# The columns of 27 tiles from a second layout of x instead of from TensorE's transposes, and the context's scans ahead of the mask's last part

## The reference, cut to what matters

```python
def _layernorm(x):  return (x - mean(x)) / sqrt(var(x) + 1e-5)
def rmsnorm(x, g):  return x * rsqrt(mean(x*x) + 1e-5) * g

e = _layernorm(x)
h = rmsnorm(e, g_res) @ W_in + b_in                 # 4096 x 512
p = rmsnorm(ctx, g_init)[:, :512]                   # 3202 x 512
s[i] = a * s[i-1] + b * p[i]                        # a scan over 3202 rows
x = x + h + s[plug]                                 # plug: rows picked by the mask's running sum
x = x + gelu(_layernorm(x) @ w1 + b1) @ w2 + b2     # 512 -> 2048 -> 512
```

## Time and profile before

| | us |
|---|---|
| median of 3 runs | 851.08 (849.31 to 851.92) |
| the profiled execution, its own time | 849.29 |
| its span | 847.6 |
| TensorE busy / VectorE / ScalarE / GpSimd | 833.6 / 318.0 / 286.9 / 254.7 |
| matmuls of the second phase | 3072 |
| share of the chain that ended last: TensorE / VectorE / DMA | 88% / 5% / 3% |

### The profile page before, as it was taken

One profiled execution on the slowest core, in us unless ns is written; L12 is line 12 of the kernel. 1 busy time (PEld: TensorE's weight loads), 2 busy tenths in 40 slices (PEclk: granted clock), 3 DMA queues, 4 the chain that ended last, 5 costly groups with the idle time before them and its releaser, 6 DMA issues.

```text
span 847.6 us, 10756 instructions
## 1 busy us (share of the span) xinstructions
PE 833.6 (98%) x3786; PEld 684.8 (81%) x3786; DVE 318.0 (38%) x511; ACT 286.9 (34%) x522; POOL 254.7 (30%) x236
## 2 busy tenths in 40 slices
PE   7999989999999999999999999999999999999998
PEld 5887868888888888888888887888888888888886
DVE  5899762534342333324152425133113311242112
ACT  4674335442532244222622253222222322222221
POOL 2273365970262016300532053203500250001000
PEclk9999999999999999999999999999999999999999
DMA  9877687170215021331215021502300140010001
GB/s 233 253 205 217 218 242 253 49 172 1 74 51 156 16 74 51 93 79 49 73 49 124 0 74 49 97 0 100 50 0 1 50 97 2 0 50 0 1 1 50
DMA packets 34968, 71.07 MB, mean 84 GB/s; under 512 B 5716, under 2 KB 5716, under 8 KB 33176
## 3 DMA queue, kind: packets, MB, share of 16 engines
q1 hardware_dynamic: 25964, 58.91, 21.6%
q0 software_dynamic: 4608, 8.39, 6.3%
q10 hardware_dynamic: 4368, 3.42, 1.3%
HBM read 47.87 MB, written 22.84 MB: 83 GB/s over the span
## 4 chain that ended last, share of the span: by engine, by line
PE 88%; DVE 5%; DMA 3%; SPq 1%; issue 1%; POOL 1%; ACT 0%; DVEq 0%; POOLq 0%; ACTq 0%
PE acc L841 14%; PE acc L842 14%; PE acc L843 14%; PE h_bank L842 14%; PE h_bank L843 14%; PE h_bank L841 14%; DMA xa_odd<-in_x_dram 2%; PE t_bank L900 2%; DMA x_next<-scan_table,idx 1%; DVE h_lo L1023 1%; DVE st_a L1018 1%; DVE cl L1037 1%; POOL x_next L541 1%; DVE xa_odd L1031 1%; PE t_bank L873 1%
## 5 line engine op out<-in xcount | busy, mean ns | idle before, releaser
L1242 DVE TENSOR_TENSOR h_lo<-g_f,h_hi 128x512 fp32r<-128x512 f32 x128 | 101.3, 791 | 449.6 <-ACT g_f L778 440.1
L776 ACT ACTIVATE h_hi<-h_bank,b_c 128x512 fp32r<-128x512 f32 x128 | 88.1, 689 | 441.1 <-PE h_bank L843 436.2
L841 PE MATMUL h_bank<-xt_hi,w_hi 128*128 128x512 f32 x512 | 201.9, 394 | 0.0
L841 PE MATMUL acc<-w_hi,h_hi 128*128 128x512 f32 x512 | 199.8, 390 | 0.0
L843 PE MATMUL h_bank<-xt_hi,w_lo 128*128 128x512 f32 x512 | 199.4, 389 | 0.0
L842 PE MATMUL h_bank<-xt_lo,w_hi 128*128 128x512 f32 x512 | 199.3, 389 | 0.0
L843 PE MATMUL acc<-w_hi,h_lo 128*128 128x512 f32 x512 | 199.2, 389 | 0.0
L842 PE MATMUL acc<-w_lo,h_hi 128*128 128x512 f32 x512 | 199.2, 389 | 0.0
L841 PEld LDWEIGHTS h_bank<-xt_hi,w_hi 128*128 128x128 f32 x512 | 96.1, 188 | 20.9 <-issue 1.2
L842 PEld LDWEIGHTS h_bank<-xt_lo,w_hi 128*128 128x128 f32 x512 | 96.1, 188 | 20.8 <-issue 1.2
L843 PEld LDWEIGHTS h_bank<-xt_hi,w_lo 128*128 128x128 f32 x512 | 96.1, 188 | 20.1
(11 more groups left out here) (164 smaller groups left out, 698.5 us busy)
## 6 DMA issues: line engine op xcount, KB each, us to landing
out_dram<-x_cur SPq DMA_DIRECT2D x32, 256.0 KB, 2.1
x_next<-x_part SPq DMA_DIRECT2D x7, 1024.0 KB, 4.8
w_raw<-in_L_ffn_w_dram SPq DMA_DIRECT2D x6, 1024.0 KB, 8.8
scan_table<-cl SPq DMA_DIRECT2D x6, 896.0 KB
ch<-in_ctx_dram SPq DMA_DIRECT2D x20, 256.0 KB
cl<-in_ctx_dram SPq DMA_DIRECT2D x5, 1024.0 KB
xa_even<-in_x_dram SPq DMA_DIRECT2D x16, 256.0 KB, 6.1
xa_odd<-in_x_dram SPq DMA_DIRECT2D x16, 256.0 KB, 6.8
```

The costliest lines, as they stand in the source:

```text
L776: act.activation(h_hi[:, m % HB, :], h_bank[m % 2][:], ACT.Gelu, bias=b1_c[:, m:m + 1])
L841: nc.tensor.matmul(dst, a_hi, b_hi, start=first, stop=False)
L1242: dve.tensor_tensor(h_lo[:, m % HB, :], g_f32[:], h_hi[:, m % HB, :].bitcast(F32), ALU.subtract).then_inc(h_split, 1)
```

## The change

Tiles 5 to 31 are no longer turned by TensorE. The host hands over a second array `x_cols` in which each tile of x lies already turned, and `load_tile` loads it in front of the tile's rows, 256 KB more for each tile, into 12 slots (`xc`) in the part of `w_raw` where the weight quarters 1 to 3 come later. ScalarE and the subtraction read the slot in SBUF in place of the bank in PSUM. For the odd tiles 5 to 21 the subtraction is done by GpSimd (`tile_low` there, 9 tiles). The scans and carries are in iterations 12 to 18, the second half of `oh_p`, `count_rows` and `finish_plug` in 14, 17 and 19. The block stores are in 17 and 20, the gather in GpSimd's iteration 22 behind `scales(24)`, the quarter 0 weights in 15 and 18. At the start ScalarE issues two parts of W_in ahead of `g_res`, and W_in's first low part is ahead of tile 1's.

```diff
+def from_host(t):
+    return t >= 5
+def low_on_pool(t):
+    return t % 2 == 1 and 5 <= t < 22
...
+        def xc(t):
+            u = HOSTED.index(t) % XTR
+            q = 3 - u // K
+            return w_raw[:, u % K, q * D:(q + 1) * D]
...
+        def wait_low(engine, t):
+            if low_on_pool(t):
+                engine.wait_ge(xc_lo, POOL_LOW.index(t) + 1)
+            else:
+                engine.wait_ge(x_lo, DVE_LOW.index(t) + 1)
...
             def load_tile(t):
+                if from_host(t):
+                    m = HOSTED.index(t)
+                    if m >= XTR:
+                        wait_low(sp, HOSTED[m - XTR])
+                        sp.nop(nofuse=True)
+                    sp.dma_start(xc(t), x_cols[t, :, :]).then_inc(xc_loaded[m % XTR], 16)
                 sp.dma_start(xa(t), x_v[t // TI, :, t % TI, :]).then_inc(xa_loaded[t % XR], 16)
...
+            def tile_low(t):
+                pool.wait_ge(x_hi, t + 1)
+                pool.tensor_tensor(h_lo[:, t % HB, :], xc(t), h_hi[:, t % HB, :].bitcast(F32), ALU.subtract).then_inc(xc_lo, 1)
...
             for t in range(NT):
+                if t + 2 < NT and low_on_pool(t + 2):
+                    tile_low(t + 2)
...
-                if t % TI == TI - 1 and t < 24:
+                if t % TI == TI - 1 and t < 22:
                     scales(t + 1, TI)
+                if t == 22:
+                    scales(24, TI)
+                    wait_apart(pool, table_stored, STORED + BLOCK_STORED * 2)
+                    for i in range(TI):
+                        add_context(0, i, 2)
                 if t == 24:
                     scales(28, TI)
...
             def tile_high(t):
-                act.wait_ge(x_turned, t + 1)
                 if t >= HB:
                     act.wait_ge(h_used, t - HB + 1)
-                act.activation(h_hi[:, t % HB, :], first_bank[t % 3][:], ACT.Copy).then_inc(x_hi, 1)
+                if from_host(t):
+                    m = HOSTED.index(t)
+                    act.wait_ge(xc_loaded[m % XTR], 16 * (m // XTR) + 16)
+                    act.activation(h_hi[:, t % HB, :], xc(t), ACT.Copy).then_inc(x_hi, 1)
...
             for t in range(3, NT):
-                if t + 2 < NT:
+                if t + 2 < NT and not from_host(t + 2):
                     transpose_first(t + 2)
...
-                if t == 14:
-                    count_positions()
-                if t == 16:
-                    count_before()
+                if t == 15:
                     pe.wait_ge(consts_made, 5)
                     carry(0, cl, acc[3][:])
-                if t == 19:
-                    pe.wait_ge(plug_ready, 1)
-                    carry(1, cl_next, h_bank[0][:])
+                if t == 16:
+                    count_positions()
+                if t == 18:
+                    count_before()
+                    pe.wait_ge(block_ready, 1)
+                    carry(1, cl_next, acc[3][:])
...
-                if 2 <= t < NT - 2:
+                if 2 <= t < NT - 2 and not low_on_pool(t + 2):
                     tile_low(t + 2)
...
+    laid['x_cols'] = _np.asarray(inputs['x']).reshape(NG, P, TI, K, P).transpose(0, 2, 4, 3, 1).reshape(NT, P, D)
```

More of the change, by code:

```diff
@@ L106, in stats_made, with xattn_ffn @@
     return sum(1 for v in tiles if v < t)
-def xattn_ffn(nc, x, ctx, mask, w_in, b_in, g_res, g_init, w1, b1, w2, b2, out):
+def from_host(t):
+    return t >= 5
+def low_on_pool(t):
+    return t % 2 == 1 and 5 <= t < 22
+TURNED = [t for t in range(NT) if not from_host(t)]
+HOSTED = [t for t in range(NT) if from_host(t)]
+POOL_LOW = [t for t in range(NT) if low_on_pool(t)]
+DVE_LOW = [t for t in range(NT) if not low_on_pool(t)]
+XTR = 12
+def xattn_ffn(nc, x, x_cols, ctx, mask, w_in, b_in, g_res, g_init, w1, b1, w2, b2, out):
     x_v = x.rearrange("b (g p i) d -> (b g) p i d", p=P, i=TI)
@@ L195, in last_turned @@
         def last_turned(i):
-            return max(t for t in range(NT) if t % 3 == i) + 1
+            return max(t for n, t in enumerate(TURNED) if n % 3 == i)
         b_in_b = sb("b_in_b", [P, D])
@@ L298, in xattn_ffn @@
         x_lo = sem("x_lo")
+        xc_lo = sem("xc_lo")
+        xc_loaded = [sem(f"xc_loaded{i}") for i in range(XTR)]
         n_b_ready = sem("n_b_ready")
@@ L413, in _ @@
                     loaded += 1
-                if t == 18:
+                if t == 17:
+                    store_block(0, cl)
+                if t == 20:
+                    store_block(1, cl_next)
+                if t == 22:
                     load_high_half(NA, 0)
                     load_high_half(NA, 1)
[L417 to L421, removed]
+                if t == 25:
                     wait_apart(sp, table_stored, STORED + BLOCK_STORED * 2)
@@ L575, in _ @@
                     add_bias(t - 14)
-                if t == 18:
+                if t == 20:
                     pool.wait_ge(plug_ready, 1)
                     gather_indices(0)
-            wait_apart(pool, table_stored, STORED + BLOCK_STORED * 2)
-            for i in range(TI):
-                add_context(0, i, 2)
             for k in range(K):
@@ L637, in _ @@
             own = Tally(act_self)
+            for k in range(2):
+                act.dma_start(win_raw[:, k, :], win_v[:, k, :]).then_inc(win_loaded[k], 16)
             act.dma_start(g_res_c[:], g_res.rearrange("(k p) -> p k", p=P),
                           allow_slow_non_contiguous=True).then_inc(g_res_loaded, 16)
-            for k in range(2):
-                act.dma_start(win_raw[:, k, :], win_v[:, k, :]).then_inc(win_loaded[k], 16)
             act.sem_inc(gelu_done, CREDIT)
@@ L665, in tile_high @@
             def tile_high(t):
-                act.wait_ge(x_turned, t + 1)
                 if t >= HB:
                     act.wait_ge(h_used, t - HB + 1)
-                act.activation(h_hi[:, t % HB, :], first_bank[t % 3][:], ACT.Copy).then_inc(x_hi, 1)
+                if from_host(t):
+                    m = HOSTED.index(t)
+                    act.wait_ge(xc_loaded[m % XTR], 16 * (m // XTR) + 16)
+                    act.activation(h_hi[:, t % HB, :], xc(t), ACT.Copy).then_inc(x_hi, 1)
+                else:
+                    act.wait_ge(x_turned, TURNED.index(t) + 1)
+                    act.activation(h_hi[:, t % HB, :], turned_bank(t)[:], ACT.Copy).then_inc(x_hi, 1)
             def tile_stats(t):
@@ L1022, in tile_low @@
                 dve.wait_ge(x_hi, t + 1)
-                dve.tensor_tensor(h_lo[:, t % HB, :], first_bank[t % 3][:], h_hi[:, t % HB, :].bitcast(F32),
+                dve.tensor_tensor(h_lo[:, t % HB, :], xc(t) if from_host(t) else turned_bank(t)[:], h_hi[:, t % HB, :].bitcast(F32),
                                   ALU.subtract).then_inc(x_lo, 1)
@@ L1303 @@
     arrays, args = {}, []
+    laid = dict(inputs)
+    laid['L0_xattn_W_in'] = _np.asarray(inputs['L0_xattn_W_in']).T
+    laid['x_cols'] = _np.asarray(inputs['x']).reshape(NG, P, TI, K, P).transpose(0, 2, 4, 3, 1).reshape(NT, P, D)
     for name in _INS:
-        a = _np.ascontiguousarray(inputs[name].T if name == 'L0_xattn_W_in' else inputs[name])
+        a = _np.ascontiguousarray(laid[name])
         arrays[f"in_{name}_dram"] = a
```

58 lines of the change are left out of this document (31 added, 27 removed).

## The result

| | before | changed |
|---|---|---|
| median (13 runs each) | 850.78 us | 853.76 us |
| lowest to highest | 848.60 to 852.73 | 852.05 to 856.85 |
| span of the profiled execution | 847.6 | 850.7 |
| second phase's first matmul | 128.31 | 131.58 |

The ratio is 1.0042, 95% interval 1.0033 to 1.0051: slower by a little more than the 0.3% that can be told apart here, where 841 us and "faster" had been forecast. From the second phase's first matmul to the end both take 719 us (847.6 - 128.31, 850.7 - 131.58), so all of it lies in the first phase.

The account below looks back on a forecast made before the run. TensorE's instruction count was taken to bound both phases, with VectorE nearly as full. Tile 22 unchanged at 90.0, then 7.6 us saved plus 1.7 for the clock: 9.3 off 849.3 gives 840.0, 841 as median; range 833 to 850.

Parts of the forecast that it names:

- The transposes: TensorE in the first phase: 27 sets of four transposes at 0.48 us go, 13.0 us off its path.
- The loads, early: Six added tile loads (1.57 MB) ahead of tile 10's rows cost 4.1 us at the good stretch's 386 GB/s.
- VectorE, the middle, and the port: VectorE from tile 8 to iteration 20: 46.6 us instead of 48.2, starting at 38.9; port conflicts with GpSimd add 2 us.
- +2 for tile 22: Allowance for VectorE stalls at the SBUF port shared with GpSimd, moving tile 22's start from 88.0 to 90.0.
- The count of 28 instructions: About 28 VectorE instructions with two SBUF operands in the middle piece, stalls bounded between 0 and 18 us.
- counting back from iteration 20: From VectorE's iteration 20 at 85.5, less what is left of iterations 17 to 19 (0.9 + 3.7 + 4.7): row_tot at 76.2.
- the 88.0: Tile 22's start before the port: tile 18 at 77.1, then four periods of 2.72 us.
- The end of the phase: Tile 22 to n_rows' transposes: 21.8 us instead of 29.4; n_rows wait 0 to 1 us instead of 4.0.
- the 1.7 us of the clock: Low TensorE clock after the n_rows wait costs 1.7 us before; forecast to be won as that wait shrinks.
- the forecast's 90.0: Tile 22 starts at 90.0, as before (89.98), all that the transposes gave being spent by then.
- the 9.3 forecast: Total gain: 7.6 us from tile 22 to n_rows' transposes, and 1.7 for the clock.
- Rival 3: Port decides: 28 VectorE instructions wait 0.9 us more each, low parts late, tile 22 at 102, 853 to 856; chance 0.09.

Follow-up runs that it names:

- r3: Changed kernel with the second context block's two loads (2 MB) behind tile 11 on SyncE's queue instead of ahead of tile 10: 851.22 us, ratio 1.0022.
- e5: Changed kernel with g_init given its own semaphore, so GpSimd's first product need not wait for b1: 855.21 us, ratio 1.0048.
- e6: Changed kernel with g_init's own semaphore and the second context block's loads behind tile 11: 848.46 us, ratio 0.998.
- r1: Changed kernel with GpSimd's nine low parts of tiles 5 to 21 back on VectorE: 855.76 us, ratio 1.0059.
- z3: z1 with all low parts on VectorE, tiles still hosted: 847.19 us, ratio 0.9969.
- z2: z1 with nothing hosted, TensorE turning every tile, and all low parts on VectorE: 842.01 us, ratio 0.9913.
- z1: e6 with count_before moved to iteration 20, second carry and finish_plug one iteration later, block 1's store earlier, at 18: 845.60 us, ratio 0.9952.
- e8: Kernel before the change with only the gather issued ahead of the scales of tiles 28 to 31: 847.44 us, ratio 0.9964.

## Why the forecast was wrong, step by step

**The transposes**: right. 13 us left TensorE's path, and tiles are 2.72 us apart from 22 on.

**The loads, early**: right to 0.4 us. ScalarE waited for tile 10 until 34.91 (34.85 forecast) and at the good rate, 388 GB/s. Tile 7's high part came at 36.62 (36.5), tile 8's low part at 39.16 (38.9); tile 7 was projected from 38.6 (38.2). What the sum left out is that the same full DMA engines held up the small vectors too: GpSimd's first product started at 41.82, and at 34.55 before; r3, e5 and e6 show 2 us for tile 10's rows alone, nothing for this alone and 5.3 us for both.

**VectorE, the middle, and the port**: the steps that failed. `row_tot` was forecast for 76.2 and done at 86.2. Of these 10.0 us, 6.8 are stretches at the port (11.6 less 4.8), where the sum had +2 for tile 22. The count of 28 instructions took only those with two operands in SBUF; but casts, copies and `tensor_scalar` with one operand are stretched as well, 26 or 8 elements to 0.77 to 1.22 us, and GpSimd's products, held up by the small vectors' loads, fell among them. Another 1.8 are a slip in counting back from iteration 20: between `row_tot` and it lie 7.5 us of VectorE's work, not 9.3. The last 1.1 are VectorE's later start (39.16 for 38.9) and a wait of 0.85 us for tile 16's high part. This is arithmetic on the trace: no run took all the stretches away. r1 took 3.5 us of them away and paid 4.8 for it.

The Trainium skill, "SBUF — State Buffer", section "Who interferes with whom", names copy, cast and `tensor_scalar` beside the two-operand kind as able to take the shared port. The trace agrees, with the rows above; the prediction had read the rule for one kind alone.

**A clock after the waits**: missing in the sum. From tile 18 to 22 are 13.3 us where four periods are 10.9, and the count and carry ahead took 2.0 instead of 0.9: 3.5 us. With the 10.0 that makes 101.5 out of the 88.0 that the sum had ahead of its +2.

**The end of the phase**: right. 22.8 us (21.8), the wait 0.87 (0 to 1), and 3.70 us from the transposes to the next instead of 5.30, so the 1.7 us of the clock were won.

So tile 22 is 11.5 us later than the forecast's 90.0 and the end 1.0 longer: 12.5, and 12.5 less the 9.3 forecast is 3.2, the 3.1 by which the span grew. **Rival 3** gave this number, tile 22 at 102 and 853 to 856, for half the cause: instructions at the port were stretched and low parts came late (TensorE waited 6.0 us for GpSimd's), but by 7 us more than before and not 14, and r1 shows that moving the subtractions back doesn't help. That its number was met is partly luck: the slip of 1.8 and the 3.5 of count, carry and clock, which it didn't have, made up for most of the rest. Its chance of 0.09 was too small for what the rows of the kernel before showed of one-operand instructions: a cast (0.35 us at 40.52) and an integer `tensor_scalar` (1.27 us at 44.36), both 0.17 by themselves, were stretched there too.

The prediction did count TensorE, and asked of each wait how long it would be; it never asked how much of the 13 us could be used if VectorE's list, with the table's additions and tile 27's statistics in it, came no sooner. The runs answer: with hosting that list comes later, not sooner (z3 against z2), and in the best order found, which waits for nothing without hosting, none of the 13 us was gained.

## What to carry to other kernels

Before work is taken off the busiest engine, follow the longest chain of results through the other engines to the point where this engine waits for them, and compare its end with the time at which the engine would be there: z2 is fast because the result is there at about 113.2 and the engine at 113.6. A result that is late is best asked for later (z1 against e6: 5.96 us of waiting gone with `count_before`, one carry and `finish_plug` an iteration or two later, though with the block's store moved as well the time fell by only 2.4 us, since the wait for `n_rows` grew from 1.77 to 3.96), and a TensorE that stands for 4 us pays about 2 us again in clock (1.7 before, 2.5 in z1). Traffic and port time that the relief needs fall on the engines that carry the chain; price them there.

## What the runs showed of the hardware

- A one-operand VectorE instruction of 26 elements, 0.18 us by itself, takes 1.22 us beside a GpSimd product and ends within 0.04 us of it (f32 `tensor_scalar`, changed kernel at 43.19); a cast of 26 elements from int32 to f32 takes 0.77 and a copy of 8 elements 1.15 us, both 0.17 or 0.18 by themselves.
- A load of 8 KB (`b1`) takes 20.9 us from issue to landing behind and beside the x tiles, and a product on GpSimd that didn't need it waited for it through a shared semaphore.
- After TensorE's waits of 5.92 us (changed kernel) and 3.96 us (z1) the granted clock was 0.59 and 0.60 in the stretches shown, the lower level of 1.2 GHz for most of them; after e5's wait of 2.38 us it was 0.72 from 126 to 132 us; after e8's wait of 1.96 us and the changed kernel's 0.87 us it stayed at 1.00, the full 2.4 GHz.
